# Attention inside a four-stage kernel: the Q/K projections and the other side work move between the score uses

## What is computed

```python
n_heads = 16                      # head_dim = 16, L = 1024, B = 8
qkv = (x @ Wqkv + bqkv).reshape(B, L, 3, n_heads, head_dim)       # x is layer-normalized
q, k, v = (qkv[:, :, 0], qkv[:, :, 1], qkv[:, :, 2])
scores = jnp.einsum('bqhd,bkhd->bhqk', q, k) / math.sqrt(head_dim)
scores = scores + slopes[None, :, None, None] * bias[None, None]  # bias = -|i - j|
probs = jax.nn.softmax(scores, axis=-1)
out = jnp.einsum('bhqk,bkhd->bqhd', probs, v).reshape(B, L, D)
return out @ Wout + bout
```

## Time and profile before

| | |
|---|---|
| time, median of three runs (range) | 3262.87 us (3258.28 to 3268.13) |
| the profiled execution: its time, its span | 3271.27 us, 3269.5 us |
| granted TensorE clock, mean over the span | 0.952 |
| busy over the span: PE, DVE, ACT, POOL | 3085.7, 2534.6, 1985.8, 1094.2 us |
| first and last exponential of attention (L1855) start at | 1250.1 us, 2918.4 us |
| exponentials x mean duration | 1024 x 1027 ns |

### The profile page before, as it was taken

The page is one execution under the profiler, slowest core; times in us unless marked ns, Lnnn a source line. Parts: engine busy times, 40 slices in busy tenths (PEclk is TensorE's granted clock), DMA queues, the critical chain, the costliest instruction groups (busy, mean ns, idle before and its releaser), DMA issues. The chain is left out here.

```text
span 3269.5 us, 73440 instructions
## 1 busy us (share of the span) xinstructions
PE 3085.7 (94%) x28196; PEld 1827.7 (56%) x28196; DVE 2534.6 (78%) x5875; ACT 1985.8 (61%) x2967; POOL 1094.2 (33%) x1364
## 2 busy tenths in 40 slices
PE   7999999995999869999999999999999999988999
PEld 3666666664788734444454444444544445437888
DVE  6677877764788658888888889788888887927887
ACT  2455444441666515777777777767777777775665
POOL 3354554443223221332423333323233232222222
PEclk8899999985999958999999999999999999998999
DMA  1000000002111151324232323232322322202111
GB/s 54 2 28 28 28 28 28 20 10 73 66 59 59 39 108 36 58 39 83 40 67 55 57 63 60 43 77 52 71 48 49 74 49 53 57 18 93 52 60 38
DMA packets 126461, 165.34 MB, mean 51 GB/s; under 512 B 23584, under 2 KB 104240, under 8 KB 125456
## 3 DMA queue, kind: packets, MB, share of 16 engines
q1 hardware_dynamic: 115688, 149.37, 18.7%
q0 software_dynamic: 9984, 10.38, 2.4%
q10 hardware_dynamic: 440, 0.90, 0.1%
HBM read 81.58 MB, written 38.24 MB: 37 GB/s over the span
## 5 line engine op out<-in xcount | busy, mean ns | idle before, releaser
L1855 ACT ACTIVATE b_p_t<-banks 128x1024 f32<-128x1024 f32 x1024 | 1040.2, 1027 | 304.0 <-PE banks L1742 238.7
L1681 PE MATMUL banks<-b_k_stack,b_q_stack 62*128 62x512 f32 x2048 | 809.6, 475 | 26.5 <-issue 10.8
L1742 PE MATMUL banks<-b_q_stack,b_k_stack 64*128 64x512 f32 x2048 | 767.8, 450 | 9.9 <-ACT b_p_t L1855 9.9
L1941 DVE CUSTOM_DVE_ANT_1 banks<-banks,b_near_rows 128x512 f32<-128x512 f32 x960 | 649.0, 715 | 138.3 <-PE banks L1681 135.1
L1944 DVE TENSOR_REDUCE b_half_max<-banks 128x1 f32<-128x512 f32 x1024 | 657.8, 684 | 79.9 <-PE banks L1681 76.3
L1696 PE MATMUL banks<-b_p_t,b_v 128*17 128x256 f32 x8192 | 631.8, 386 | 6.3 <-POOL b_p_t L2100 5.5
L1742 PEld LDWEIGHTS banks<-b_q_stack,b_k_stack 64*128 64x128 f32 x2048 | 313.7, 185 | 389.1 <-issue 325.5
L2100 POOL TENSOR_TENSOR b_p_t<-b_p_t,b_fall 128x256 f32<-128x256 f32 x384 | 280.5, 733 | 658.6 <-ACT b_p_t L1855 657.8
L1681 PEld LDWEIGHTS banks<-b_k_stack,b_q_stack 62*128 62x128 f32 x2048 | 341.9, 188 | 111.6 <-DVE b_half_max L1941 35.9
L1696 PEld LDWEIGHTS banks<-b_p_t,b_v 128*17 128x17 f32 x8192 | 142.8, 95 | 300.7 <-issue 162.2
L1148 ACT ACTIVATE ffn_relu<-banks,ffn_scale_fc 128x512 f32<-128x512 f32 x256 | 176.2, 688 | 205.5 <-PE banks L1080 205.5
(11 more groups left out here) (255 smaller groups left out, 5333.6 us busy)
## 6 DMA issues: line engine op xcount, KB each, us to landing
ffn_x<-x SPq DMA_DIRECT2D x32, 512.0 KB, 3.9
b_q_stack<-b_qk_hi SPq DMA_DIRECT2D x252, 64.0 KB
b_k_stack<-b_qk_hi SPq DMA_DIRECT2D x252, 64.0 KB
b_fall<-c_fall SPq DMA_DIRECT2D x48, 256.0 KB, 2.6
a_x<-hidden_states SPq DMA_DIRECT2D x16, 512.0 KB, 3.9
x<-a_x SPq DMA_DIRECT2D x16, 512.0 KB, 2.9
x<-ffn_x SPq DMA_DIRECT2D x16, 512.0 KB, 2.8
b_x<-x SPq DMA_DIRECT2D x8, 1024.0 KB, 5.6
```

The source lines that it names most:

```text
L1681: pe.matmul(m, q_stack[rows, slot, qb * P:(qb + 1) * P], k_stack[rows, slot, half * BANK:(half + 1) * BANK], start=True, stop=True, tile_p ...
L1742: last = pe.matmul(out, k_stack[stack, slot, kb * P:(kb + 1) * P], q_stack[stack, slot, half * BANK:(half + 1) * BANK], start=True, stop=n ...
L1855: act.activation(p_t[use % P_BUFS][:, :, :], scores[use % 2], ACT.Exp, scale=slopes()[pair][0]).then_inc(p_made, 1)
L1941: dve.tensor_tensor_reduce(out=m, in0=m, in1=near_window(pair, qb, rg), scale=1.0, scalar=LOWEST, op0=ALU.add, op1=ALU.max, accum_out=larg ...
```

## The change

- Every engine's `attend` yields once for a use instead of once for each of its two matmuls, so that side work stands between uses.
- `make_stacks` takes a half. Half 0 of group g + 2 stands between uses 3 and 4; half 1 is made a group earlier, for group g + 3, between uses 19 and 20 (`GAPS`).
- ACT reads a projection's bank once, into `qk`; POOL makes `qk_hi` (a new cast of 128x512) and `qk_lo`.
- The maxima's transpose stands behind row turn 3 instead of before turn 2, the negated copy moves from ACT to DVE at turn 4, POOL's split and SP's transfers move from turn 3 to turn 5, which is one use later.
- Values and output projection work on two tiles at a time with one bank (512 columns), one read-out for two; the buffers `att_hi`, `att_lo`, `y` are single and twice as wide. The transposes of a pair now stand a step before its products.
- `normalize` has weight 2: its nine steps lie in the first half of the group.
- SP issues the four `k_bias` transfers ahead of its wait for `qk_lo`, and the heads in the order of their use.

The diff, cut to its core:

```diff
+        att_hi, att_lo = (sb(f"att_{part}", [P, KT, 2 * P], F32R) for part in ("hi", "lo"))
+        y = sb("y", [P, 2, DIM])
...
-        STEPS, STACKS, VALUES, NORMALIZE = GROUP * HALVES * QB, 2, QB, 1 + QB
-        LEAD, TURN = 16, 2
+        STEPS, STACKS, VALUES, NORMALIZE = GROUP * HALVES * QB, 12, QB // 2, 1 + QB
+        GAPS = (1, 7)
+        LEAD, TURN = 16, 4
...
-                side_by_side(*([(STEPS, attend(g, rows), 1)] if g >= 0 else []),
+                side_by_side(*([(STEPS // ROWGROUPS, attend(g, rows), 1)] if g >= 0 else []),
                              *([(STEPS + LEAD, lead(), 1)] if g == -1 else []),
-                             *([(STACKS, stacks(g + 2), 3)] if 0 <= g + 2 < ALL else []),
+                             *([(STACKS, stacks(g + 2, 0), 1)] if 0 <= g + 2 < ALL else []),
+                             *([(STACKS, stacks(g + 3, 1), 1)] if 0 <= g + 3 < ALL else []),
                              *([(VALUES, make_values(b), 1)] if last and b < BATCH else []),
-                             *([(NORMALIZE, normalize(b), 1)] if g % GROUPS == 1 and b < BATCH else []))
+                             *([(NORMALIZE, normalize(b), 2)] if g % GROUPS == 1 and b < BATCH else []))
...
@@ tensor, find_maxima @@
-                    if g and turn == TURN:
+                    if g and turn == TURN - 1:
                         m, (used, n) = misc.take(("turn", g - 1), (shift_copied, g))
...
@@ scalar, make_stacks @@
-                    act.activation(qk_hi[:, cols], m, ACT.Identity, bias=b_scaled[:, hg:hg + 1],
-                                   scale=scale_qk[:, 0:1]).then_inc(qk_hi_made, 1)
-                    act.activation(qk[:, cols], m, ACT.Identity, bias=b_scaled[:, hg:hg + 1],
-                                   scale=scale_qk[:, 0:1]).then_inc(qk_made, 1)
+                        act.activation(qk[:, cols], misc.at["qk", g, half], ACT.Identity, bias=b_scaled[:, hg:hg + 1],
+                                       scale=scale_qk[:, 0:1]).then_inc(qk_made, 1)
...
@@ scalar, find_maxima @@
-                        act.activation(shift_full[:, :], m, ACT.Copy, scale=-1.0).then_inc(shift_copied, 1)
@@ vector, find_maxima @@
+                    if g and turn == TURN:
+                        dve.wait_ge(max_turned, g)
+                        if g >= 2:
+                            dve.wait_ge(shift_made, g - 1)
+                        dve.tensor_scalar(shift_full[:, :], misc.at["turn", g - 1][0:2 * GROUP * QB, 0:P], -1.0, None, ALU.mult).then_inc(shift_copied, 1)
...
@@ gpsimd, make_stacks @@
+            def make_stacks(g, half):
+                for step in range(STACKS):
+                    if step == GAPS[half]:
+                        use, cols = 2 * g + 1 - half, slice(half * BANK, (half + 1) * BANK)
+                        pool.wait_ge(qk_made, use + 1)
+                        if g:
+                            for i in range(GROUP):
+                                pool.wait_ge(stacked[slot_of(g - 1) + i], 112 * ((g - 1) // SETS + 1))
+                        pool.tensor_copy(qk_hi[:, cols], qk[:, cols]).then_inc(qk_hi_made, 1)
+                        pool.wait_ge(qk_hi_made, use + 1)
+                        pool.tensor_tensor(qk_lo[:, cols], qk[:, cols], qk_hi[:, cols].bitcast(F32), ALU.subtract).then_inc(qk_lo_made, 1)
                     yield
...
@@ every engine, attend @@
                     if rg == ROWGROUPS - 1:
                         follow(t, pair)
-                    yield
+                        yield
```

243 lines of the change are left out of this document (123 added, 120 removed).

## The result

Four runs of the changed kernel took 3219.19 us in the median (3216.07 to 3224.77), and the kernel before, on the same chip, 3260.57 us (3249.4 to 3268.13). The ratio is 0.9882, with a 95% interval of 0.9851 to 0.9913: faster by 1.2%, 41 us, where 76 us were forecast. The profiled execution took 3216.07 us (span 3214.3 us).

The account below looks back on a forecast made before the run. PE and DVE were both taken as full, at 1.22 and 1.23 us a use. Group gains of 2.5, 2.2, 2.4 and 3.0 make 10.1 us a batch element, 76 us over 7.5: 3262.9 to 3187 us, range 3168 to 3208.

Parts of the forecast that it names:

- Plain group: Group with only its two Q/K projections: 44.4 us forecast against 46.8, a gain of 2.4 us.
- 3.2 for the projections: Two projections in a plain group cost only PE's own 1.59 us each, 3.2 instead of 4.2 us.
- 1.2 for the transposes: Transposes of the weighed values in a plain group, 0.58 us twice, kept at 1.2 us.
- 0.3 of small waits: Small waits at the two halves' beginnings in a plain group fall from 0.9 to about 0.3 us.
- The shift: Group's end: later split leaves a wait of some 0.4 us in part of the groups; nothing added, bounds 0 and 1.2.
- The turn: Turning the maxima: no wait for the transpose; DVE's copy and maxima cost PE about 0.6; 1.5 becomes 0.7 us.
- Output projection: Groups with index mod 4 = 0: pairs net nothing, DVE waits 0.4 us a step for att_hi; gain 2.5 us.
- Normalization: Groups with index mod 4 = 1: statistics wait 2.7 and POOL's chain 1.2, together 3.9 instead of 1.9; gain 2.2 us.
- Values: Groups with index mod 4 = 3: plain gain 2.4 plus 0.6 from tiles in pairs, 3.0 us.
- Rival 2: Projections starve DVE, which passes the gaps on: plain group 45.2 us and more, kernel 3220 us; chance 0.20.
- Rival 3: PE's longer statistics wait halves its clock in all seven normalization groups: 10 us, 3197; no separate chance, inside the forecast's range.
- Rival 4: Slower: late qk transfers hold POOL at use 20, delaying multiplications from use 24 and all weighing; chance 0.05.

Follow-up runs that it names:

- The first experiment: Also x1_shift: the changed kernel with POOL's split and SP's transfers of the shift at row turn 4 instead of 5; 3206.26 us, ratio 0.9847.
- the last one: Also x11_late: the kernel of experiment 9 with POOL's split and SP's transfers of the shift at turn 5 again; 3176.11 us, ratio 0.9754.
- experiment 11: The changed kernel with the shift at turn 4 and the negated copy of the maxima on ACT again; 3206.49 us, ratio 0.9846.
- experiment 3: Also x3_single: the changed kernel with the output projection in single tiles, as in the kernel before; 3208.34 us, ratio 0.9855.
- experiment 7: Also x6_ahead: the changed kernel with output-projection pairs whose transposes stand ahead of the previous pair's products, att_hi and att_lo doubled; 3193.33 us, ratio 0.9812.
- experiment 8: Also x7_best: the changed kernel with shift at turn 4, single-tile output projection, normalize behind the half-0 projection with one more idle step; 3182.04 us, ratio 0.9767.
- experiment 9: Also x8_all: the kernel of experiment 8, but output projection two tiles at a time with the transposes ahead; 3162.03 us, ratio 0.9707.

## Why the prediction was right, and where it was too large

The direction, the range and the mechanism of the main part hold; the gain was about half of the forecast, 41 us of 76. By its steps:

- **Plain group, 44.4 forecast, 45.46 measured.** The beginnings of the halves are right in sum. Uses 2 to 4 last 5.86 us, 2.20 over three undisturbed uses, and uses 18 to 20 5.91, 2.25 over: together 4.45, where 3.2 for the projections, 1.2 for the transposes and 0.3 of small waits were counted, 4.7. That this sum is nearly met is partly luck, as its parts are different: in a half that has no projection (group 29 with the earlier shift) these three uses last 4.68, so that a projection costs 1.19 us in the gap, less than its own 1.59, and the bare beginning costs 1.0. The 1.06 us by which the group is longer than forecast are the shift (0.59), the turn (0.27 more than forecast) and nearly 0.1 us above 1.22 in each of uses 6, 8, 22 and 24, which the sum didn't have, less the 0.25 of the beginnings; 0.1 is left unexplained.
- **The shift, "I add nothing".** This step failed: it is 0.59 us in plain and 0.68 in normalization groups, not made up by anything. The forecast expected a wait of some 0.4 us in part of the groups and put nothing in the sum, because DVE would work off a backlog meanwhile; that reason didn't hold. The range of 0 to 1.2 took it in. The size follows from one figure: the split was counted 1.22 us later, and it is 2.11 later, as the use between the two multiplications is the turn's. 1.5 us of slack less 2.1 are the 0.6 that were missing. The first experiment shows the cost, and the last one again.
- **The turn, 0.7.** It is 0.97 us in the changed kernel (uses 25 and 26, 3.41 us). DVE's copy, which the forecast blamed with the maxima, is not what costs (experiment 11). Which of the others it is (the maxima of 0.23 us, the extra bank of the ring) was not tried.
- **Output projection, "net nothing" on top of the plain gain.** Failed in its size: DVE's wait was put at 0.4 us a step, and it was near 2 in the four long ones. By the lengths, this group has the 1.9 us that a plain group gains without the shift's wait, and the pairs take 0.7 of them back. Single tiles (experiment 3) or another order in the step (experiment 7) end that.
- **Normalization, 3.9 us for statistics and chain.** PE's wait of 2.7 us and its place were right. The 1.2 us for POOL's chain didn't come: PE doesn't wait for `xn` in any group. Missing in the sum was the price of the dip on the projection behind the wait, which it had as a rival only (a dip of 3.4 us costs 1.4 us by experiments 8 and 9), and that the group's end waits for the shift. 54.5 us instead of 51.6.
- **Values, 3.0.** The total was met by luck. It was counted as 2.4 of the plain gain and 0.6 of its own. Measured without the shift's wait, which doesn't reach this group, the plain gain is 1.9 (46.82 to 44.93), and the values' own part fell from 7.2 to 6.1 us over a plain group, 1.1. No experiment was made on the pairs of values alone.
- **The rivals.** Rival 2 named the time that came out, 3220, and a plain group of 45.2 or more, but not for its reason: with the shift's wait gone the plain group is 44.93, and the projection in the gap costs less than PE's own time, though DVE stands 0.97 us beside it (group 14), where the forecast had well under 1. Rival 3 came true: a dip in each normalization group. The Trainium skill (TensorE: Matmul & The Clock Gate, HAM oscillation) tells of a kernel in which PE's waits for its inputs bring the half clock back each time; the trace agrees for the waits of 2.7 us here, which are shorter than that kernel's. It doesn't settle the waits of 0.73 us, which were followed by a dip in one kernel, by none in another, and in two groups of six in x11_late: the length of the wait alone doesn't decide. Rival 4 didn't come: PE's weighing matmuls waited for POOL 1.3 us in all.
- **What gains.** For the projections it is the place: two reads instead of one change nothing in a plain group, the turn alone gives 0.3%, and the same code with the projections three uses later is slower than the kernel before. That values in pairs gain as well is read from the groups' lengths only.

**What stays open.** Three kernels that differ in other groups by 0.5 to 1.0 us (changed, x1_shift, x3_single) kept a batch element at 207.9 to 208.1 us, and their dips stood 208.2 us apart. It looks as if the dips held the period. x6_ahead speaks against it: its output groups are 2.3 us shorter, its batch element is 206.4, and its dips stand 204.8 and 208.2 us apart in turn, long ones and short ones. What the records do show is that the length of a dip goes with its place in the group. First a short and a long dip of x1_shift (groups 5 and 9), then two of x6_ahead (groups 9 and 13):

```profile
1488.60:1492.00 3.40, 3.38 (x10) 2.68 (x10) 1.18 (x4) 1.36 (x2) 3.04 (x5) 0.50 0.00 0
1693.40:1700.20 6.80, 6.54 (x23) 3.63 (x23) 3.40 (x10) 2.35 (x3) 5.08 (x7) 0.50 0.00 0
```

```profile
1689.30:1692.70 3.40, 3.40 (x16) 1.72 (x16) 2.65 (x8) 1.62 (x2) 3.32 (x5) 0.50 0.00 0
1894.10:1900.90 6.80, 6.50 (x23) 3.63 (x23) 3.44 (x10) 2.30 (x3) 5.10 (x7) 0.50 0.00 1
```

In the six kernels with a wait of 2.7 us and the projections in the gap, every dip that began 3.8 to 5.0 us into its group lasted 6.8 us, and every one that began 5.3 us or more into it 3.4 us. A gain in the other groups shifts where the dips fall in the normalization group, and where they then begin earlier in it, 1.1 us of the gain is lost in each. In the fastest kernel, which has no dips, nothing is taken back. No run here shows how a dip's place is chosen, or why x8_all has none where x7_best has one in each group.

## What to carry to other kernels

Side work between two saturated engines is cheapest where one of them has a natural hole, and it should be placed by what stands behind it on all engines: here the same projection costs 1.2 us in the gap and 2.1 us three uses on. When a chain with a transfer is moved a step later, the step has to be taken as long as it is at that place (here 2.1 us, not the usual 1.2), its slack has to be counted to the consumer's first instruction, and a shortfall should be entered as a cost. A measured edit may show nothing because a longer clock dip elsewhere takes it back; groups have to be compared kind by kind, those with equal dips with each other, and edits tried together. A total that comes out right is to be split into its terms as well.
